# Decoder layer on one core: seven-product gate and up for batch 2 as well, silu issued later, recurrence of batch 3 moved, first q and k interleaved

## What is computed

```python
kqv = x @ Wqkv + bqkv                      # 16 heads of 32; the first third is q, then k, v
scores = einsum('bsnh,btnh->bnst', k, q) / sqrt(32)
scores = triu(scores) + -10000.0 * tril(ones, k=-1)
attn = softmax(scores, axis=2)             # over the first token axis
x = layernorm(x + (einsum('bnkq,bknh->bqnh', attn, v).reshape(...) @ Wo + bo))
x = layernorm(x + wkv(w, u, k=x, v=ctx))   # a recurrence over the 512 tokens, by channel
Wg, Wu, Wd = (q - 128) * scale             # int32 weights 0..63, 2048 inner features
x = layernorm(x + (silu(x @ Wg.T) * (x @ Wu.T)) @ Wd.T)
```

## Time and profile before

| | us |
|---|---|
| median of 3 runs | 721.95 |
| lowest, highest | 720.39, 724.36 |
| the profiled execution's own time | 722.09 |
| its span, first to last instruction | 720.3 |
| mean granted TensorE clock | 0.994 of full |

### The profile page before, as it was taken

One profiled execution on the slowest core, in us unless ns is written; L12 is line 12 of the kernel. 1 busy time (PEld: TensorE's weight loads), 2 busy tenths in 40 slices (PEclk: granted clock), 3 DMA queues, 4 the chain that ended last, 5 costly groups with the idle time before them and its releaser, 6 DMA issues.

```text
span 720.3 us, 12504 instructions
## 1 busy us (share of the span) xinstructions
PE 702.0 (97%) x4466; PEld 409.7 (57%) x4466; DVE 538.6 (75%) x1224; ACT 443.4 (62%) x1037; POOL 307.0 (43%) x345
## 2 busy tenths in 40 slices
PE   8998999999999999999999999999999999999997
PEld 3465556666655666565655455444545444568855
DVE  3588666789999989889944789866767687557744
ACT  5579867779888788678775764245423653336620
POOL 2014331374575423651244864375534774104421
PEclk9999999999999999999999999999999999999999
DMA  7725745473233233354008001000000000010001
GB/s 234 227 85 167 230 122 132 103 214 100 53 118 117 75 89 120 96 114 126 2 6 171 1 18 57 30 15 0 1 16 29 15 1 1 15 46 2 1 15 45
DMA packets 45534, 54.21 MB, mean 75 GB/s; under 512 B 4896, under 2 KB 34848, under 8 KB 45472
## 3 DMA queue, kind: packets, MB, share of 16 engines
q1 hardware_dynamic: 41632, 46.59, 20.9%
q0 software_dynamic: 3264, 6.29, 5.1%
q10 hardware_dynamic: 576, 0.52, 0.3%
HBM read 47.10 MB, written 12.58 MB: 83 GB/s over the span
## 4 chain that ended last, share of the span: by engine, by line
PE 85%; DVE 4%; ACT 4%; issue 3%; DMA 3%; POOL 1%; SPq 1%; ACTq 0%; POOLq 0%; DVEq 0%
PE psb L1022 23%; PE psb L910 9%; PE psb L1073 7%; PE psb L1071 7%; PE psb L948 7%; PE psb L1049 7%; PE psb L993 5%; PE psb L926 5%; PE psb L961 4%; PE psb L937 4%; PE psb L1009 3%; PE psb L981 2%; PE psb L972 2%; DVE ee L1383 1%; ACT ee L1162 1%
## 5 line engine op out<-in xcount | busy, mean ns | idle before, releaser
L1383 DVE CUSTOM_DVE_ANT_0 ee<-psb,mask,clip 128x512 f32<-128x512 f32 (+3 forms) x256 | 130.5, 535 | 23.2 <-PE psb L937 22.3
L1162 ACT ACTIVATE ee<-ee,nm 128x512 f32<-128x512 f32 (+3 forms) x256 | 141.8, 558 | 1.4 <-DVE nm L1383 1.4
L1774 POOL TENSOR_TENSOR hl<-ring,hh 128x512 f16<-128x512 f32 x64 | 78.2, 1227 | 90.0 <-ACT hh L1297 58.5
L1173 ACT ACTIVATE ee<-psb 128x256 f32<-128x256 f32 (+1 forms) x160 | 83.7, 531 | 41.4 <-PE psb L948 36.9
L948 PE MATMUL psb<-ident,ee 128*128 128x128 f32 x640 | 99.6, 274 | 3.3 <-ACT ee L1173 1.9
L1071 PE MATMUL psb<-wd,hh 128*128 128x512 f16 x240 | 91.0, 379 | 0.0
L1073 PE MATMUL psb<-wd,hl 128*128 128x512 f16 x240 | 91.0, 379 | 0.0
L948 PEld LDWEIGHTS psb<-ident,ee 128*128 128x128 f32 x640 | 75.1, 141 | 24.5 <-ACT ee L1173 4.3
L1297 ACT ACTIVATE hh<-ring 128x512 bf16<-128x512 f32 x48 | 30.2, 630 | 80.4 <-DVE ring L1509 75.9
L937 PE MATMUL psb<-ks,qs 128*128 128x512 f16 (+3 forms) x256 | 73.7, 301 | 4.9 <-DVE nm L1383 3.3
L1022 PE MATMUL psb<-x2h,wu 128*128 128x512 f16 x192 | 72.8, 379 | 0.0
(11 more groups left out here) (187 smaller groups left out, 1442.5 us busy)
## 6 DMA issues: line engine op xcount, KB each, us to landing
qs<-parts SPq DMA_DIRECT2D x64, 128.0 KB, 2.7
ks<-parts SPq DMA_DIRECT2D x60, 128.0 KB, 3.3
parts<-qhl SPq DMA_DIRECT2D x16, 256.0 KB, 2.1
parts<-khl SPq DMA_DIRECT2D x16, 256.0 KB, 2.1
x<-in_x SPq DMA_DIRECT2D x4, 1024.0 KB, 6.5
ct<-in_ctxT SPq DMA_DIRECT2D x4, 1024.0 KB, 5.0
out<-x SPq DMA_DIRECT2D x16, 256.0 KB, 2.0
xt<-in_xT SPq DMA_DIRECT2D x14, 256.0 KB, 3.4
```

Of the source, the lines that this page charges most:

```text
L1162: e.activation(dst, dst, ACT.Exp, bias=NM[:, n % 4, col:col + 1], scale=-1.0, accum_out=DEN[:, n % 4, col:col + 1]).then_inc(sem("exp"), 1)
L1173: e.activation(ET[h][:, base:base + width], PSB[:, bank["turn", H, item], 0:width], ACT.Copy).then_inc(sem("et"), 1)
L1383: e.tensor_tensor_reduce(E[H % 3][:, EOFF[i]:EOFF[i] + w], PSB[:, bank["score", H, i], 0:w], MASK[:, S - w:S], -SC, CLIP[:, i:i + 1], ALU. ...
L1774: e.tensor_tensor(HS[it][1][:], pair(b, it // 2)[:, it % 2, :] if b in SEVEN else ring(b, it)[1], HS[it][0][:], ALU.subtract).then_inc(sem ...
```

## The change

- `SEVEN` becomes (2, 3): gate and up of batch 2 are computed by seven products too.
- The silu of pair m - 1 is issued after snap5 of pair m, and its `hfb` after c11 of pair m; before, both stood at the end of pair m - 1. The last pair of a batch keeps its place.
- `first_qk` and `qk_high`: x's pieces are taken one by one, each with the high and low weights of q and of k; then the low parts of x by q's weights, and by k's. The weights of k are loaded second. `split_w` 2 follows the high and low parts of q, and `split_w` 3 those of k.
- The recurrence of batch 3, all weight sums, and the input sums of batch 2 have new slots. All other tables have new values as well: places of q, k, v, `wo`, loads and splits, the delays `WAIT`, and which engine does the copies (`COPIES`), `oh` (`OH_POOL`), the splits of x (`XH_POOL`) and the product of `EK` with the context (`KEYS`).

The core of the diff (tables of attention that keep their character are cut):

```diff
-SEVEN = (3,)
+SEVEN = (2, 3)
...
-W_SPLIT = (7, 8, 9, 15)
-V0_AT = (0, 9)
-QK_AT = {2: (8, 17), 3: (10, 27), 4: (40, 51), 5: (57, 63), 6: (67, 75), 7: (80, 87), 8: (105, 113), 9: (124, 131),
-         10: (136, 144), 11: (146, 151), 12: (166, 175), 13: (173, 195), 14: (194, 202), 15: (212, 228)}
+W_SPLIT = (9, 10, 11, 21)
+V0_AT = (3, 13)
+QK_AT = {2: (12, 16), 3: (19, 25), 4: (38, 44), 5: (45, 55), 6: (70, 76), 7: (75, 84), 8: (103, 112), 9: (124, 128),
+         10: (131, 136), 11: (144, 152), 12: (171, 174), 13: (174, 195), 14: (203, 205), 15: (216, 222)}
...
-WG_ZERO = (226, 233, 241, 244)
+WG_ZERO = (222, 229, 241, 242)
...
-WKV_AT = {(0, 0): 111, (0, 1): 123, (0, 2): 133, (0, 3): 143, (1, 0): 191, (1, 1): 209, (1, 2): 262, (1, 3): 264,
-          (2, 0): 267, (2, 1): 272, (2, 2): 275, (2, 3): 277, (3, 0): 289, (3, 1): 294, (3, 2): 296, (3, 3): 301}
-YT_AT = {0: (156, 164, 174, 183), 1: (270, 270, 270, 270), 2: (284, 285, 286, 287), 3: (306, 306, 310, 310)}
-X2_AT = {0: (225, 228, 230, 233), 1: (272, 272, 272, 272), 2: (290, 291, 294, 294), 3: (313, 313, 313, 313)}
+WKV_AT = {(0, 0): 111, (0, 1): 123, (0, 2): 134, (0, 3): 144, (1, 0): 193, (1, 1): 208, (1, 2): 262, (1, 3): 264,
+          (2, 0): 266, (2, 1): 271, (2, 2): 274, (2, 3): 276, (3, 0): 283, (3, 1): 289, (3, 2): 291, (3, 3): 294}
+YT_AT = {0: (158, 166, 167, 179), 1: (268, 268, 269, 269), 2: (281, 283, 286, 288), 3: (300, 301, 303, 304)}
+X2_AT = {0: (224, 226, 228, 230), 1: (272, 274, 274, 274), 2: (292, 292, 292, 292), 3: (312, 312, 312, 313)}
...
-WS_AT = {1: (284, 291), 2: (289, 301), 3: (307, 307), 4: (304, 306)}
+WS_AT = {1: (276, 279), 2: (280, 283), 3: (276, 279), 4: (287, 291)}
...
-KEYS = (0, 0, 0, 0)
-
-TURN = ((4, 6, 5), (3, 4, 6), (3, 6, 5), (3, 4, 4))
-
-OH_POOL = (0, 0, 0, 1, 1, 1, 0, 0, 0, 0, 1, 0, 0, 1, 0, 0)
-XH_POOL = (0, 1, 1, 0)
-
-COPIES = (5, 2, 0, 4, 1, 1, 0, 0, 0, 0, 0, 2, 0, 0, 0, 1)
+KEYS = (1, 0, 0, 0)
+
+TURN = ((7, 6, 5), (4, 5, 7), (4, 5, 6), (2, 4, 4))
+
+OH_POOL = (1, 1, 1, 1, 1, 1, 0, 0, 0, 0, 0, 0, 1, 1, 0, 0)
+XH_POOL = (0, 1, 0, 1)
+
+COPIES = (0, 0, 0, 0, 6, 0, 0, 0, 0, 0, 0, 0, 4, 0, 0, 3)
...
+    def first_qk():
+
+        for kind in "qk":
+            tt.unit("qk", 0, kind)
+            tt.unfinished.add(("qk", 0, kind))
+        add("qk_high")
+        for kind in "qk":
+            add("qk", 0, kind, 2)
+            tt.unfinished.discard(("qk", 0, kind))
+            add("high", 0, kind)
+            add("low", 0, kind)
+            add("put", 0, kind)
+            tick()
+            add("split_w", 2 if kind == "q" else 3)
+        add("split_w", 4)
+        add("stack", 0)
...
             if j == 2:
                 add("c11", b, m)
+                gated(b, m - 1)
             else:
                 add(f"snap{j}", b, m)
+            if j == 5:
+                silus(b, m - 1)
+
+    def silus(b, m):
+        for it in (2 * m, 2 * m + 1) if m >= 0 else ():
+            add("silu", b, it)
+
+    def gated(b, m):
+        for it in (2 * m, 2 * m + 1) if m >= 0 else ():
+            add("hfb", b, it)
...
-        for it in (2 * m, 2 * m + 1):
-            add("silu", b, it)
+        if m == PAIRS - 1:
+            silus(b, m)
...
-        for it in (2 * m, 2 * m + 1):
-            add("hfb", b, it)
+        if m == PAIRS - 1:
+            gated(b, m)
...
+        def qk_high():
+
+            for k in range(T):
+                for low in (0, 1):
+                    for kind in "qk":
...
+                        e.matmul(PSB[:, bank["qk", 0, kind], :], WQK[0][low][:, k, c0:c0 + P], xh[:, k, :],
+                                 start=(k == 0 and low == 0), stop=False)
...
                 load_w(0)
+                load_w(1)
                 for k in (1, 2, 3):
                     load_x(0, k)
-                load_w(1)
```

More of the change, by code:

```diff
@@ L73 @@
           14: (4, 2, 13)}
 LAST_AT = (5, 5, 6)
-WAIT = {'high': 1, 'low': 1, 'vtake': 1, 'r1': 2, 'norm': 4, 'exp': 4, 'eb': 0, 't1': 0, 't3': 0, 'oh': 2, 'ol': 2,
-        'ek': 1, 'scan_q': 3, 'scan_p': 6, 'divide': 8, 'r2': 2, 'x2h': 1, 'x2l': 2, 'expand': 0}
-WAIT_IN = {'norm2': 5, 'r1': 6, 'norm': 1, 'ek': 0, 'scan_q': 1, 'scan_p': 1, 'divide': 2, 'r2': 0, 'x2h': 1, 'x2l': 2}
-PIECE_AT = {'load_second': 43, 'small': 102, 'split_wo': 46, 'load_ds': 228}
-WU_AT = (53, 74, 79, 119)
-WU_ZERO = (85, 85, 135, 142)
@@ L92 @@
-YT_AT = {0: (156, 164, 174, 183), 1: (270, 270, 270, 270), 2: (284, 285, 286, 287), 3: (306, 306, 310, 310)}
-X2_AT = {0: (225, 228, 230, 233), 1: (272, 272, 272, 272), 2: (290, 291, 294, 294), 3: (313, 313, 313, 313)}
-WO_IN = (8, 8, 12, 13)
-ZERO_IN = (5, 7, 7, 7, 8, 9, 10, 10, 12, 14, 14, 14, 14, 14, 14, 14)
-WS_AT = {1: (284, 291), 2: (289, 301), 3: (307, 307), 4: (304, 306)}
+WAIT = {'high': 1, 'low': 1, 'vtake': 1, 'r1': 2, 'norm': 6, 'exp': 4, 'eb': 0, 't1': 1, 't3': 0, 'oh': 2, 'ol': 3,
+        'ek': 1, 'scan_q': 2, 'scan_p': 7, 'divide': 8, 'r2': 3, 'x2h': 0, 'x2l': 3, 'expand': 0}
@@ new lines @@
+WAIT_IN = {'r1': 0, 'norm': 2, 'ek': 0, 'scan_q': 1, 'scan_p': 1, 'divide': 2, 'r2': 0, 'x2h': 0, 'x2l': 2,
+           'norm2': 5}
+PIECE_AT = {'load_second': 37, 'small': 82, 'split_wo': 46, 'load_ds': 185}
+WU_AT = (49, 56, 56, 59)
+WU_ZERO = (56, 124, 127, 150)
+WG_AT = (205, 221, 226, 229)
+WG_ZERO = (222, 229, 241, 242)
+REST_AT = (0, 25, 104, 15)
+BO_AT = (55, 104, 130, 177)
+XLOAD = {1: (0, 0, 18, 24), 2: (57, 61, 80, 85), 3: (131, 142, 151, 163)}
+XSPLIT = {1: (19, 26, 32, 34), 2: (83, 89, 91, 98), 3: (150, 153, 159, 169)}
@@ L432, in timetable @@
     add("split_w", 0)
+    add("split_w", 1)
     for k in (1, 2, 3):
         add("split_x", 0, k)
-    add("split_w", 1)
     add("scale_bqk")
-    first, second, vs0 = qk_units(0), qk_units(1), v_units(0)
-    for u in first[:3]:
-        u()
-    add("split_w", 2)
-    add("split_w", 3)
+    second, vs0 = qk_units(1), v_units(0)
+    first_qk()
     tick()
-    for u in first[3:]:
-        u()
     tick()
@@ L913, in qk @@
                 mm.then_inc(sem("qk"), 1)
+        def qk_high():
+            for k in range(T):
+                for low in (0, 1):
+                    for kind in "qk":
+                        part = PART_OF[kind, 0]
+                        if low:
+                            pe.wait_ge(*by("split_w", part))
+                        else:
+                            pe.wait_ge(sem("wh"), done["split_w", part])
+                            pe.wait_ge(*by("split_x", 0, k))
+                        c0 = P * "qk".index(kind)
+                        e.matmul(PSB[:, bank["qk", 0, kind], :], WQK[0][low][:, k, c0:c0 + P], xh[:, k, :],
+                                 start=(k == 0 and low == 0), stop=False)
         def v(b, t, p):
@@ L1084, in _ @@
                 qk(*a)
+            elif name == "qk_high":
+                qk_high()
             elif name == "v":
```

21 lines of the change are left out of this document (8 added, 13 removed).

## The result

The changed kernel takes 718.7 us, the median of 20 runs (716.99 to 720.85), against 721.5 us for the kernel before beside it (20 runs, 718.76 to 726.24). The ratio is 0.9963, interval 0.9949 to 0.9977: 2.8 us faster, where 7 were forecast. The profiled execution took 719.11 us with a span of 717.3.

A forecast was written before the change was run, and what follows sets the result against it. TensorE's matmuls were taken to bound the kernel, without waits from about 380 us and with small leaks in attention. From 722.09 us, -6.2 + 0.4 - 0.8 - 0.5 + 0 = -7.1 gave 715.0 us, range 709 to 720.

The forecast's parts named there:

- the paid backlog: Rival: VectorE's full list in batch 1 makes TensorE wait some 3 us there and in batch 2's first pairs; 718 us, chance 0.15.
- Part 1: Batch 2's gate and up: 448 matmuls of 256 columns replace 256 of 512, 49.1 us instead of 55.3, minus 6.2 us.
- The rival of matmuls that don't get cheaper by half: Batch 2's gate and up: half the columns cost 0.72 of the price, plus 14.4 us; 735 us, chance 0.01.
- Part 2: Batches 1 and 2: helper engines, chiefly VectorE, nearly keep up with TensorE; plus 0.4 us, bounds 0 to plus 4.
- The slower rival: VectorE bounds batch 1, its waits for GpSimd and ScalarE no longer free, costing 10 us; 724.5 us, chance 0.04.
- Batch 2's input sums: Asked for at slot 292, in batch 1's down product; three down products hide them, so they cost nothing.
- The silu's place, a guard in batch 2: Moved silu keeps a late c12 from holding up the next pair's snap1 and snap5; worth nothing in batch 3.
- Part 3: Start, first q and k together: minus 0.8 us up to k's high part, minus 0.5 from there to first score.
- The second term: From k's high part to first score: v's matmuls leave a slow-clock stretch; minus 0.5 us, bounds 0 to minus 1.5.
- Part 4: Attention tables: TensorE's work unchanged, ScalarE's load grows as VectorE's falls; 0 us, bounds minus 5 to plus 3.
- the rival in which ScalarE bounds the early heads: Slots 16 to 40 take 3 us more at ScalarE's pace and the start gives nothing; about 719 us, chance 0.06.

## Why the prediction was wrong

The direction and the range held; the forecast of 715.0 us was 3.7 too low, and the rival that came true is the second one, the paid backlog at 718 us, to which I gave 0.15. That its number is so near is partly luck: it had 3 us of waits where 6.5 came, and nothing from the attention part, which gave 1.9.

- **Part 1, minus 6.2: right.** It shows wherever the waits are away. The stage without seven products is 57.00 us; with them and with the reciprocals out of the way it is 53.79 with 2.95 us of stops, so 50.8 without them, 6.2 less. The rival of matmuls that don't get cheaper by half is dead.
- **Part 2, plus 0.4: this is the step that failed.** It measured plus 6.5, beyond its upper bound of 4. The load was counted well: about 87 us less 5 of overlap for VectorE in batch 1, against 53.54 + 28.83 = 82.4. The tolerance of some 4 us was sound too: without a stop, pair 1's p6 is due at 548.4 + 9 x 0.876 = 556.3 us; less `snap1`'s 0.6 and `c11`'s 0.6 this lets `c11` start until 555.1, 4 us behind p2, whose end is due at 551.0. It started at 559.85. It was the path that was wrong, too: the prediction looked for TensorE's stops at p7 (through `c12` and `snap6`) and at p4 (through `c22`), and 5.1 of the 6.5 us stand before p6, through `c11` and `snap1`. What was wrong was to put full TensorE in batch 2 of the kernel before beside it as evidence. Plain gate and up have banks between VectorE and TensorE; the first pairs of seven products have one `snap` buffer, and what counts there is what stands in front of one instruction. The prediction never wrote down that row of instructions: the scans (2.4 us), the wait for GpSimd (2.75), three reciprocals (2.6), the residual and its statistics (2.4), a fourth reciprocal (0.9), then `c11`. Putting the reciprocals behind `c11` took 3.5 us of the 6.5 away. The 1.8 us before pair 0's p6 stayed; their cause, the late third tile and the slow shift, is read from the timelines and not tried.
- **The slower rival's mechanism was half right.** It had the wait for GpSimd in a full list, 2.2 us each, and its counter that a late VectorE finds most of what it waits for done. This holds up to the last chunk, where VectorE waits 2.75 us: its reciprocals stand right behind the scans whose results GpSimd needs first, and GpSimd was busy with batch 1's `rs` and `shift` until 551.3 us.
- **Batch 2's input sums, "nothing": too low.** Three down products hide them from batch 2's first product, as said. But they keep VectorE for 2.8 us and the low parts for 4.1 (L1563 and L887), where I had 4 in all, and the reciprocals of chunk 2 and batch 1's last three residuals stand behind them. That this is why VectorE reached the third tile at 545.96, some 4.7 us late, is read from the timeline; no run took the sums away.
- **The silu's place, a guard in batch 2: right,** and its price without was 4.8 us. The mechanism is the one given, with two things on top that I had not counted: the table load of 1.28 us, and 2.8 us that matmuls lose at the low clock behind the longer stop.
- **Part 3, minus 0.8 and minus 0.5: right in sum between the two profiles, and partly by luck.** The first score came 1.34 us earlier, and k's high part started at 12.65 where 12.8 was worked out for the full clock. But the old order at the full clock has its first score at 21.84, only 0.6 us behind the new order's average, so about 1.1 of the 1.34 can be the low clock in the profile of the kernel before. The 1.3 us that undoing it cost in the median do not confirm the term, as the profile of that run loses nothing before batch 2. The second term's reason was not seen as such: the clock of 24 to 28 us is half in some profiles of either order and full in others.
- **Part 4, 0: too cautious by 1.9 us.** The waits for the row maximum fell from 3.3 to 1.3 us; they were never most of the 5.3 us of idle between 20 and 90, as the prediction read them, but 1.6 of it. ScalarE's busy time between 20 and 90 us is 57.9 as forecast (58), and TensorE's waits for its copies there fell from 1.2 to 0.9 us, so nothing of the rival in which ScalarE bounds the early heads shows. Which of the tables did it wasn't tried apart, and the size moves with the clock: from the first score to batch 1's first gate the new tables take 436.7 to 437.5 us in the profiles with the full clock from 24 to 28 us, and 438.3 to 438.6 in the others; the second profile of the kernel before, with the full clock there, has 439.9.

The sum by measured terms: -6.2 + 6.5 - 1.3 - 1.9 = -2.9 us, which is the 2.8 of the medians. Had part 2 been right, the sum would be 713.1 us, within the forecast's 712.5 to 717.

What stays open: whether an earlier place of batch 2's input sums would return the 2 to 3 us of stops that are left after the order was mended (1.82 us before pair 0's or 1.46 before pair 2's p6, depending on the norm's place); what the order of the first q and k is worth by itself; and why the clock fell behind a stop of 3.34 us in one execution and not in the other.

## What to carry to other kernels

When a helper engine's list gets full, don't compare its sum with the stage's length. Find the first instruction there that the bounding engine needs soon, and write out what stands in front of it in its queue, with each wait for a third engine; then put work whose operands come late behind it. Before moving work to another engine, look for the last place where the full engine waited for the bounding one: work taken away ahead of it is worth nothing. A wait that an edit removes is only gained if the sum of waits falls; compare the stage's length, as the releaser seen in the queue may be merely the last in a row. And when a stage is longer than its waits explain, look at the granted clock behind the longest stop before giving the rest to the edit.
